# Gated cross-attention and expert block: the maximum pass over steps 0 to 12, the row maxima transposed in step 15

## What is computed

```python
qh = layernorm(x) @ Wq.T / 4          # 16 heads of 16
kh, vh = ctx @ Wk.T, ctx @ Wv.T
scores = qh @ kh.T + rel              # rel: 9 relative distances, clipped at +-4
scores = where(q >= k, scores, -1e30)
attn = softmax(scores)                # subtracts each row's maximum
x = x + tanh(g_xattn) * (attn @ vh) @ Wo.T
x = x + tanh(g_ffn) * experts(layernorm(x))    # 8 routed experts, 4 chosen, and a shared one
```

## Time and profile before

| | us |
|---|---|
| median of 3 runs (lowest to highest) | 733.62 (731.25 to 735.79) |
| the profiled execution's own time | 733.69 |
| its span | 731.8 |
| PE, DVE, ACT, POOL busy | 618.5, 441.6, 277.4, 202.4 |
| start, to the first transposed score | 58.66 |
| units 0 to 7, to the last values | 58.66 to 364.84 |
| the rest, mostly experts | to 731.8 |

### The profile page before, as it was taken

How to read it: one execution, slowest core, us unless ns; L and a number is a source line. 1 busy time by engine, 2 the same in 40 slices (tenths; PEclk the granted TensorE clock), 3 DMA queues, 4 the chain that set the end, 5 groups by cost and what they waited for, 6 DMA issues and landing times.

```text
span 731.8 us, 10675 instructions
## 1 busy us (share of the span) xinstructions
PE 618.5 (85%) x3384; PEld 484.1 (66%) x3384; DVE 441.6 (60%) x884; ACT 277.4 (38%) x505; POOL 202.4 (28%) x201
## 2 busy tenths in 40 slices
PE   2847868787878887958547999999999999999997
PEld 2726635565546654643336888888888888888886
DVE  4678639575776749620078475756657575665653
ACT  3512546245633573425142333324232233324222
POOL 3170018110631146010130223232323223232222
PEclk9978989999999999988757999999999999999999
DMA  7940043425251434471022103031211202121220
GB/s 235 251 93 8 16 111 85 115 49 125 75 125 36 95 78 101 94 260 35 14 48 73 44 28 104 15 99 46 87 57 67 77 1 100 43 87 58 74 73 29
DMA packets 40000, 58.81 MB, mean 80 GB/s; under 512 B 8000, under 2 KB 21184, under 8 KB 39936
## 3 DMA queue, kind: packets, MB, share of 16 engines
q1 hardware_dynamic: 39968, 58.41, 29.1%
HBM read 31.93 MB, written 4.85 MB: 50 GB/s over the span
## 4 chain that ended last, share of the span: by engine, by line
issue 46%; PE 22%; DVE 11%; DMA 7%; POOL 6%; SPq 5%; ACT 2%; POOLq 0%; DVEq 0%; ACTq 0%
POOL hl L1212 4%; DMA qs<-mt 4%; PE smax L921 3%; DVE mx L649 3%; PE oT L983 3%; SPq L273 2%; PE work L897 2%; PE work L866 2%; PE sT L963 2%; PE oT L987 2%; PE sT L962 2%; PE work L998 1%; DVE sx L667 1%; SPq L302 1%; DVE mx L682 1%
## 5 line engine op out<-in xcount | busy, mean ns | idle before, releaser
L533 ACT ACTIVATE ex<-sT 128x512 f32<-128x512 f32 (+1 forms) x160 | 93.2, 593 | 182.7 <-PE sT L963 142.9
L1212 POOL TENSOR_TENSOR hl<-sg,hh 128x512 fp32r<-128x512 f32 x72 | 92.8, 1290 | 241.2 <-ACT hh L1256 241.2
L1250 ACT ACTIVATE sg<-pg 128x512 f32<-128x512 f32 x72 | 43.0, 597 | 200.1 <-PE pu L1494 199.3
L649 DVE TENSOR_REDUCE mx<-smax 128x2 f32<-128x308 f32 x187 | 79.4, 470 | 60.7 <-PE smax L921 60.1
L1509 PE MATMUL py<-wxl,hh 128*128 128x256 f32 x288 | 82.0, 285 | 3.0 <-DVE x L1394 1.9
L1509 PE MATMUL py<-wxh,hl 128*128 128x256 f32 x288 | 81.0, 281 | 0.0
L1509 PE MATMUL py<-wxh,hh 128*128 128x256 f32 x288 | 80.6, 280 | 0.0
L921 PE MATMUL smax<-km,qs 96*128 96x308 f32 (+1 forms) x244 | 71.2, 348 | 10.6 <-ACT sx L516 4.5
L1382 DVE TENSOR_TENSOR sg<-cwb,sg 128x512 f32<-128x512 f32 x64 | 67.0, 1048 | 11.7 <-DMA cwb<-cwt_d 8.2
L963 PE MATMUL sT<-qs,ks 128*128 128x256 f32 (+1 forms) x128 | 55.7, 443 | 19.4 <-DMA qs<-mt 18.1
L1377 DVE TENSOR_TENSOR sg<-pu,sg 128x512 f32<-128x512 f32 x72 | 49.2, 684 | 27.8 <-ACT sg L1250 26.5
(11 more groups left out here) (156 smaller groups left out, 1159.8 us busy)
## 6 DMA issues: line engine op xcount, KB each, us to landing
cwb<-cwt_d SPq DMA_DIRECT2D x64, 256.0 KB, 3.4
qs<-qh SPq DMA_DIRECT2D x64, 128.0 KB, 2.7
qs<-ql SPq DMA_DIRECT2D x32, 128.0 KB, 2.7
at<-rden_d SPq DMA_DIRECT2D x64, 64.0 KB, 2.3
out<-x SPq DMA_DIRECT2D x8, 512.0 KB, 4.4
ks<-km SPq DMA_DIRECT2D x16, 231.0 KB, 3.1
wx<-in_wx SPq DMA_DIRECT2D x9, 384.0 KB, 6.4
x<-in_x SPq DMA_DIRECT2D x3, 1024.0 KB, 8.6
```

Source lines behind the costliest of these rows:

```text
L533: nc.scalar.activation(ex[:, g % 2, i % 5, q0:HALF], ST[i % 2][:, q0:HALF], ACT.Exp).then_inc(exp_s, 1)
L649: nc.vector.reduce_max(mx[:, m_tile(h, p), 2 * stk:2 * stk + 2], banks[q % len(banks)][:, 0:PAIR].rearrange("p (j k) -> p j k", j=2), AX_X)\
L1212: nc.gpsimd.tensor_tensor(hl[:, i % R, :], sg[:, i % R, :], hh[:, i % R, :], ALU.subtract).then_inc(hl_done, 1)
L1250: nc.scalar.activation(sg[:, i % R, :], PG[i % RG][:], ACT.Silu).then_inc(sg_s, 1)
```

## The change

- The pass has a table, `SEEK`, of how many positions a step takes. The even units' pass (for the odd unit after them) takes `(1,1,1,1,1,2,1,1,1,2,2,1,1)`, steps 0 to 12; the odd units' pass takes `(2,1,2,1,2,2,1,1,1,2,1)`, steps 0 to 10. The order of positions 4 to 7 is changed, so that part 1 of the queries is awaited at position 6 (`SECOND`).
- `minus_max` moves from step 16 to 13, `max_T` and `max_out` from 17 to 15.
- SP issues `m_stack` ahead of part 0 of the queries, and in unit 6 ahead of the weight loads.
- `transposes`, `x_hi`, `x_lo`, `queries`, `q_out`, `q_lo` and `k_hi`, `k_lo` move two steps earlier, `values_in` and `v_in` one; `normalised` is whole in step 4 instead of halves in 5 and 6.
- `tile0` goes to steps 7, 8, 9, 9 (from 9 to 12), `tile1` to 11, 12, 13, 15 (from 13, 14, 15, 17). POOL subtracts tile 0's maxima ahead of the division instead of behind it.
- `reciprocals` moves from step 8 to step 10, behind that step's maxima and `tile0`.
- `project` moves to steps 17 and 19 (in unit 7 both in 19), `residual` to 18 and 19.
- In the start, the second query projection moves behind the whole pass on PE and ACT; on DVE its `q_lo` stands before `tile0`; the copy of the maxima stands between the two halves of `tile0`, and `m_stack` ahead of the second half's queries.

```diff
+    SEEK = ((2, 1, 2, 1, 2, 2, 1, 1, 1, 2, 1), (1, 1, 1, 1, 1, 2, 1, 1, 1, 2, 2, 1, 1))
-    TILE0, TILE1 = (9, 10, 11, 12), (13, 14, 15)
+    TILE0, TILE1 = (7, 8, 9, 9), (11, 12, 13)
+    def sought(h, step):
+        return range(sum(SEEK[h][:step]), sum(SEEK[h][:step + 1]))
...
-                for g in range(NG - 1):
+                for g in range(2):
                     sp.wait_ge(st_ps, NI * u + 5 * (g + 1))
                     k_stack(g)
+            if h == 0:
+                m_stack(b, 1)
+            elif ahead:
+                m_stack(b + 1, 0)
             if ahead:
                 sp.wait_ge(work_free, NW0 + NWORK * b + Q_USE[h] + 2)
                 sp.nop().then_inc(waited, 1)
                 sp.wait_ge(st_ps, NI * u + 15)
                 q_stack(h, 0)
+            if h == 1 and ahead:
+                k_stack(2)
...
             for i in range(NI):
-                if i < NM and (h == 0 or ahead and m_tile(mh, i) >= 2):
-                    maximum(mb, mh, i)
+                for p in sought(mh, i):
+                    if h == 0 or ahead and m_tile(mh, p) >= 2:
+                        maximum(mb, mh, p)
...
-                if i == 8 and carry:
+                if i == 10 and carry:
                     reciprocals(u - 1)
...
-                if i == 17 and (h == 0 or ahead):
+                if i == 15 and (h == 0 or ahead):
                     max_T(b + h, 1 - h, b, M_USE[h])
-                if i in (16, 18) and carry:
-                    pr = (i - 16) // 2
-                    project(b - 1 + h, 1 - h, pr, b, Y_USE[h][pr])
+                if carry and i in ((19,) if h == 1 and not ahead else (17, 19)):
+                    for pr in (range(2) if h == 1 and not ahead else ((i - 17) // 2,)):
+                        project(b - 1 + h, 1 - h, pr, b, Y_USE[h] + pr)
```

More of the change, by code:

```diff
@@ L431, in near @@
                 nc.gpsimd.tensor_tensor(keys[:, half], keys[:, half], largest[:, half], ALU.subtract).then_inc(sub0_s, 1)
+            if between is not None:
+                divide(between, 0)
         def unit(b, h, carry, ahead):
@@ L545, in unit @@
                         act.wait_ge(sub_s, 3 * (b + 1))
-                    if i < NM and m_tile(0, i) < 2:
-                        near(b + 1, i)
+                    for p in sought(0, i):
+                        if m_tile(0, p) < 2:
+                            near(b + 1, p)
                 if i in (9, 14, 19):
                     raw_out(u, h, i // 5 - 1)
-                if ahead and h == 0 and i in (16, 17):
-                    k_hi(b + 1, (i - 16,))
+                if ahead and h == 0 and i in (14, 15):
+                    k_hi(b + 1, (i - 14,))
         selectors()
@@ L562, in scalar @@
                 near(0, p, M_START)
[L563 to L567, removed]
+        for part in range(2):
+            act.wait_ge(qs_in[0][part], 16 * 6)
+        q_out(1, 10)
         batches(act, unit)
@@ L776, in unit @@
                         tile1(b + 1, 3)
[L777 to L778 removed]
+                if h == 0 and ahead and i in (15, 16):
+                    k_lo(b + 1, (i - 15,))
+                if i in (18, 19):
+                    if carry:
+                        residual(b - 1 + h, 1 - h, i - 18, NW0 + Y_USE[h] + i - 18)
+                    else:
+                        unused(1, b, Y_USE[h] + i - 18)
         dve.wait_ge(x_first, 16)
@@ L812, in vector @@
                 maximum(0, 0, p, M_START)
-            if p in (7, 9):
-                q_lo(1, 10, ((p - 7) // 2,))
-            if p == 11:
-                for part in range(4):
-                    tile0(0, part)
+        q_lo(1, 10)
+        for part in range(2):
+            tile0(0, part)
         minus_max(0, 0, start=True)
         max_out(0, 0, 12, start=True)
+        for part in range(2, 4):
+            tile0(0, part)
         for part in range(4):
@@ L1006, in unit @@
                 score(b, h, i, start)
-                if i < NM and (h == 0 or ahead):
-                    for k in range(2):
-                        max_scores(b + h, 1 - h, i, k)
+                if h == 0 or ahead:
+                    for p in sought(1 - h, i):
+                        for k in range(2):
+                            max_scores(b + h, 1 - h, p, k)
                 if i in (1, 3) and carry:
```

83 lines of the change are left out of this document (35 added, 48 removed).

## The result

The changed kernel takes 744.12 us (median of 4 runs, 742.39 to 747.08) against 732.43 us (731.07 to 735.79, 4 runs) of the kernel before on the same chip: a ratio of 1.0157, 95% interval 1.0106 to 1.0207. It is slower by 1 to 2%, where 720 us was forecast. The profiled execution spans 741.7 us, against 731.8 before; nearly all of the difference, 9.9 us, lies in the units: the last one ends at 374.73 where it ended at 364.84.

The account below looks back on a forecast made before the run. PE's list was longest in every unit, DVE's not far below, with 28.9 us of stops at unit beginnings. Terms -2 - 4.3 + 0.3 - 3.4 - 5 = -14.4, rounded to -14 against 733.69: 720 us, range 704 to 737.

Parts of the forecast that it names:

- the third rival: DVE in odd units: tile0's first add stays held, +1.4 us in three odd units, 724 us; chance 0.08.
- the odd ones give back what the even ones win: Units 1 to 5: odd units 40.6 us each, even 37.7, together 197.2 against 196.9, +0.3 us.
- part 0 of the queries ... by 37.1, covered: Odd units' end: 4.0 us of issue and 2.7 to land, done by 37.1 us, so PE would not wait.
- Even units: Reciprocal ends at 21.6 us, products at 31.2; PE waits 2.7, clock costs 1.7: 37.7 us against 40.47 in unit 4.
- Odd units 3 and 5: Reciprocal ends at 23.3 us, PE waits 3.5 before the projection, clock costs 1.8: 40.6 us against 37.73 in unit 3.
- Start: Before the units: DVE's tile1 list ends near 56.7 us, so -2 us, between -4 and +1.
- Unit 7: PE does steps 17 to 19 in the 6.67 us that it stood: 30.3 us for 35.4, -5 us.
- Unit 0's named terms: Unit 0: PE list ends 1.5 us earlier, 2 us of the 6.13 wait stay; 34.3 for 38.60, given as -4.3 us.
- rival 2: Late reciprocal makes the projection wait 6 us and more: slower or no gain, 743 us, half of it 735; chance 0.18.
- Rival 1: The projection's new wait doesn't come, reciprocal early enough or chain has slack: 692 us, half of it 706; chance 0.14.

Follow-up runs that it names:

- the halved bytes: Changed kernel, reciprocals back in step 8, six DMAs of part 0 of the queries copying 256 of 512 columns inside the units: 712.58 us, 0.9694.
- the kernel with step 8 in even units: Changed kernel with the reciprocals back in step 8 in even units only, step 10 kept in odd ones: 734.09 us, 1.0002 to the kernel before.
- the kernel with step 8: Changed kernel with the reciprocals of the divisors back in step 8 in all units: 724.44 us, 0.985 to the kernel before.
- the kernel before with step 10: Kernel before with only the reciprocals moved from step 8 to step 10: 731.13 us, 0.9968.

## Why the prediction was wrong

**Right.** The mechanism was named: the head's wait goes, the projection waits instead, and the clock is lost there. The wait for the maxima's DMA went from all heads. POOL's way from the reciprocal to its start was 7.1 us, as reckoned. The wait in odd units was 2.9 to 3.2 us for 3.5, and their reciprocal came 24.0 us into the unit for 23.3. `tile0`'s additions were not held (1.46 and 1.21 us in unit 3), so the third rival fell.

**The step that failed** is "the odd ones give back what the even ones win". By it units 1 to 5 together should have cost +0.3 us and the other four places -14.7. The first cost +22.3, the others some -12.4: unit 4, forecast 2.8 us shorter than before, got 3.3 us longer, and unit 2 likewise got longer. The forecast lay 24.3 us off in the sum of its terms: 7.5 in unit 1, 12.2 in units 2 and 4, 2.3 in units 3 and 5, 2 in the start, 2.2 in units 0 and 6, less 1.9 in unit 7. The parts follow.

**Unit 1, +7.5 us against the forecast, the largest miss of one unit.** The step was "part 0 of the queries ... by 37.1, covered". It holds for a unit whose projection stops; unit 0 has no projection, so nothing gave the queue time, and PE stood 4.26 us at the first score of the pass. The stop in the head had been counted as halved by the new order (2 us of 6.13 for the maxima), and its neighbour was not asked. The clock lost (1 - 0.82) x 48.06 = 8.7 us in this unit, where I had given it 1.8. But this is the account of one unit: the run with the old order in unit 0 took 7.4 us out of unit 1 and ended only some 2 us, within the intervals, earlier.

**Even units, +6.1 each.** Three terms of one sum, all too small. The reciprocal ended at 24.9 us where I had 21.6: PE's list from step 0 to 10 lay behind 0.26, 1.61, 0.29 and 0.29 us of waits for DVE's maxima, 2.4 us that I had placed behind step 13. POOL's division took 4.51 us, not 2.5. The clock took 3.5 us ((1 - 0.92) x 43.78), not 1.7 less a half. PE meanwhile was later too, at the projection at 32.5 us rather than 28.5, which hid 4 of those; 4.11 us of wait for 2.7 stayed.

**Odd units 3 and 5, +1.1 each.** All came some 1.6 us late, `minus_max` at 29.7 for 28. PE stood for it 0.5 to 0.6 us and not 2.2, since PE was late too. The division took 3.81 us in unit 3 for the 2.5 in the sum; the wait ahead of the projection, 3.17, was near the 3.5 forecast; and the clock was 0.88, 5.0 us for 1.8. A second low stretch lies in mid-unit, where the pass waits for DVE. The forecast of DVE as the bound there was right, its cost to PE's clock was not in the sum.

**Start, 0 for -2.** DVE's list ended at 58.4 us as before, the first score started at 58.66 as before. The moved `q_lo` waited 0.66 and 0.58 us, the additions of `tile0` took 3.23 us for 2.71, with POOL at work on the distances, and that of `tile1` 1.45 for 0.66, with POOL at its subtractions. **Unit 7** gave 1.9 us more than forecast, units 0 and 6 about 1 each less.

**Sums that don't come out.** The even units' terms for the reciprocal, 16.1 + 5.3 - 0.8 + 1.3, make 21.9 and not 21.6, and 31.2 + 4.7 + 1.7 less half a microsecond makes 37.1 and not 37.7. Unit 0's named terms, 1.5 us of waits and 4.1 of the stop, make -5.6 and not -4.3. Half of rival 2's 23 us gives 731 and not 735. Put right, the forecast is some 2 us lower, and so further off.

**The rivals.** Rival 2 named 743 us and a reciprocal at 24.3 us in even units as the point from which it decides; it came at 24.9. In odd units its point, 26, was not reached, and the rest of its loss came from unit 1 and the clock, so its figure was met in part by another way. Rival 1 had 692 to 706 us without the wait; with the wait removed from units 1 to 5 it is 724. What it lacked is what stands behind: the queries' copies, which the halved bytes show to be worth 12 us, and the waits of the pass for DVE, 14.4 us. Units 1 to 5 take 205.4 us there, 8.6 more than before the change.

**Where a page bears on it.** The division took 2.51 us beside DVE's reductions and 4.51 in the same unit after, beside `k_lo` (L651), which itself took 2.22 us for the 1.50 of its twin just ahead. The Trainium skill, "SBUF — State Buffer", Who interferes with whom, says that a DVE instruction with two SBUF inputs and a GpSimd one that reads SBUF share an interface that one holds for a whole instruction. The trace agrees with that for this pair, and unit 4 of the kernel with step 8 in even units, where the division came earlier and beside one `q_lo`, has 2.52 us again. In unit 3 the division took 3.81 us beside DVE's subtractions of `tile1` (L697, L700), whose `tp` piece took 1.65 us for 0.58 in the start. With the key casts moved back `k_lo` ran beside the division as before, and it took 3.68 and 4.97 us.

## What to carry to other kernels

When a stop is taken off a path, ask which other chain ends within its length: here three chains (maxima, queries, divisors) end near a unit's end, and removing one stop brought only the distance to the next. Count the gain by unit too: the kernel with step 8 won in units 0, 6 and 7 and lost in units 1 to 5. Moving a short link (0.54 us of DVE) behind denser work is not a small edit when a 7 us way of DMAs hangs on it; start such a link as early as its input allows. And a unit that lacks one of the others' stops (unit 0) needs a reckoning of its own.

## What the runs showed of the hardware

Behind a stop the clock cost most of the stop's length once more, and not in proportion to it. Busy time in the changed kernel behind the 4.26 us stop in unit 1, in the middle of that unit, and behind the 4.11 us stop in unit 4:

```profile
98.90:105.70 6.80, 6.75 (x24) 4.20 (x25) 2.22 (x6) 3.06 (x7) 0.00 (x0) 0.50 0.44 102
120.90:127.70 6.80, 6.80 (x24) 3.87 (x23) 6.77 (x8) 1.86 (x4) 4.86 (x3) 0.62 0.05 14
...
264.30:271.10 6.80, 6.65 (x21) 5.23 (x22) 0.75 (x1) 1.43 (x3) 0.02 (x1) 0.62 0.32 64
```

The first stretch ran wholly at 1.2 GHz: 3.4 us of work lost behind a 4.26 us stop. The second lost 2.6 us with no stop longer than 1.7 us before it; the third 2.6 behind 4.11 us. A 2.84 us stop had cost 1.7 us before, and one of 6.13 us 2.8. So the low clock nearly doubled the price of a stop at worst. Behind four short waits close together (0.70, 0.40, 0.77 and 1.71 us, the last two for DVE) the clock fell as well, which I had not expected: around a 1.56 us wait by itself it stayed at 1.00, and so it did around those of 1.4 to 2.1 us for POOL in units 1, 3 and 4 of the kernel before with step 10.

DMAs issued from ACT's queue in place of SP's landed later in one kernel (4.1 us in the median for 3.1, with step 8) and about as before in the other (2.5 for 2.7, the kernel before). In both, PE waited longer for ACT's exponentials, by 4.5 and 8.0 us.
